# Four layers of cross-attention and feed-forward on one core: in the last attention, the reciprocal of the row sums and the scaling of the probabilities change places with the statistics of the next unit

## What is computed

```python
q = (hidden_states @ Wq).reshape(B, S, N_HEADS, HEAD_DIM)
k = (encoder_hidden_states @ Wk).reshape(B, S_enc, N_KV_HEADS, HEAD_DIM)
v = (encoder_hidden_states @ Wv).reshape(B, S_enc, N_KV_HEADS, HEAD_DIM)
q = rms_norm(q, q_norm_w)
k = rms_norm(k, k_norm_w)
...
scores = jnp.einsum('bqhd,bkhd->bhqk', q, k) * scale
probs = jax.nn.softmax(scores, axis=-1)
out = jnp.einsum('bhqk,bkhd->bqhd', probs, v)
...
return out @ Wo
```

## Time and profile before

| | us |
|---|---|
| median of 3 runs | 1542.64 |
| lowest and highest | 1542.45, 1543.8 |
| the profiled execution, first to last instruction (span) | 1540.9 |
| PE busy in it | 1443.8 (94%) |
| DVE, ACT, POOL busy | 895.8, 762.5, 528.4 |
| TensorE's granted clock, mean of the span | 0.985 |

### The profile page before, as it was taken

The page is one execution under the profiler, slowest core; times in us unless marked ns, Lnnn a source line. Parts: engine busy times, 40 slices in busy tenths (PEclk is TensorE's granted clock), DMA queues, the critical chain, the costliest instruction groups (busy, mean ns, idle before and its releaser), DMA issues. The chain is left out here.

```text
span 1540.9 us, 22220 instructions
## 1 busy us (share of the span) xinstructions
PE 1443.8 (94%) x6908; PEld 1036.8 (67%) x6910; DVE 895.8 (58%) x1940; ACT 762.5 (49%) x2116; POOL 528.4 (34%) x519
## 2 busy tenths in 40 slices
PE   4999998899999999999999999999968999999998
PEld 1677777777874555557787979776745666665656
DVE  7888988888875242323555454554686555553322
ACT  4888888888882211110343535343456555544210
POOL 2667677877761000000542424221111333321000
PEclk9999999999999999999999999999979999999999
DMA  5211000200007311112100000002141000001120
GB/s 198 80 41 59 8 5 1 94 1 1 1 1 291 144 57 48 54 49 76 66 1 1 1 0 9 20 1 83 37 181 45 1 1 1 1 29 34 51 64 21
DMA packets 21304, 71.65 MB, mean 47 GB/s; under 512 B 3859, under 2 KB 6291, under 8 KB 18245
## 3 DMA queue, kind: packets, MB, share of 16 engines
q1 hardware_dynamic: 12980, 57.37, 10.0%
q10 hardware_dynamic: 8208, 12.87, 2.6%
HBM read 69.01 MB, written 1.22 MB: 46 GB/s over the span
## 5 line engine op out<-in xcount | busy, mean ns | idle before, releaser
L1190 ACT ACTIVATE l0f_silu<-bank 128x512 f32<-128x512 f32 x48 | 28.6, 597 | 199.9 <-PE bank L1114 189.8
L828 POOL TENSOR_TENSOR l0a_stepped<-l0a_y,l0a_m 128x512 f32<-128x512 bf16 x64 | 74.0, 1156 | 94.4 <-DVE l0a_m L575 93.0
L1293 DVE TENSOR_TENSOR l0f_product<-l0f_silu,bank 128x512 f32<-128x512 f32 x48 | 32.9, 688 | 123.8 <-ACT l0f_silu L1190 123.7
L856 POOL TENSOR_TENSOR l0a_head_rstd<-l0a_head_var,all_minus_half 128x4 f32<-128x4 f32 x96 | 100.8, 1054 | 7.6 <-DVE l0a_head_var L597 7.6
L427 PEld LDWEIGHTS bank<-l0a_k_t,l0a_q_t 128*128 128x128 f32 x512 | 63.2, 191 | 49.1 <-ACT l0a_q_t L753 45.1
L767 ACT ACTIVATE l0a_work<-bank,l0a_neg_max 128x128 f32<-128x128 f32 x256 | 90.2, 370 | 0.9 <-DVE l0a_neg_max L610 0.9
L1126 PEld LDWEIGHTS bank<-all_weights_a,l0f_hidden 128*128 128x128 f32 x384 | 72.9, 190 | 25.2 <-issue 17.0
L1730 DVE TENSOR_TENSOR all_weights_a<-bank,all_cols 128x512 f32<-128x512 f32 x64 | 43.9, 690 | 77.9 <-PE bank L1559 45.9
L1126 PE MATMUL bank<-all_weights_a,l0f_hidden 128*128 128x256 f32 x384 | 88.9, 379 | 0.0
L427 PE MATMUL bank<-l0a_k_t,l0a_q_t 128*128 128x128 f32 x512 | 72.1, 284 | 17.1 <-ACT l0a_q_t L753 16.7
L2608 POOL TENSOR_TENSOR l3a_q_scale<-l3a_q_var,all_minus_half 128x4 f32<-128x4 f32 x32 | 32.4, 1013 | 159.7 <-DVE l3a_q_var L2398 159.7
(11 more groups left out here) (434 smaller groups left out, 3825.8 us busy)
## 6 DMA issues: line engine op xcount, KB each, us to landing
l0f_spread<-l0f_weights ACTq DMA_DIRECT2D x32, 192.0 KB, 2.7
all_weights_a<-in_l_w_q SPq DMA_DIRECT2D x2, 2048.0 KB, 14.5
l0f_spread<-l0f_weights ACTq DMA_DIRECT2D x32, 128.0 KB, 2.9
all_weights_b<-in_l_e_gate_up SPq DMA_DIRECT2D x1, 3200.0 KB, 10.6
all_weights_b<-in_l_e_gate SPq DMA_DIRECT2D x1, 3072.0 KB, 10.2
all_weights_a<-in_l_e_up SPq DMA_DIRECT2D x4, 768.0 KB, 7.2
all_weights_a<-in_l_e_down SPq DMA_DIRECT2D x1, 3072.0 KB, 16.8
l3a_spread<-l3f_weights SPq DMA_DIRECT2D x10, 256.0 KB, 3.5
```

The costliest lines, as they stand in the source:

```text
L828: done = g.tensor_tensor(stepped[:, 0:n], value, step, ALU.add)
L856: g.tensor_tensor(head_rstd[:, m % 2, :], head_var[:, m % 2, :], res.minus_half[:, 0:HU], ALU.pow)\
```

## The change

It edits the lists of two engines. On DVE, `row_inverse` of a unit is due one step earlier and stands between `keep_rows` and `variance` of the unit that follows it. On POOL, `scale_probs` is due one step earlier and stands ahead of `query_scale` of the unit that follows it.

```diff
--- before.py
+++ after.py
@@ -2510,7 +2510,7 @@
             keep_queries(0, 0)
             keep_rows(0, 1)
             march(VTS, STEPS, [(attention(row_max), later(UNIT, 2)), (attention(keep_queries, 1), later(UNIT, 1)),
-                               (attention(row_inverse), later(UNIT, 3)), (attention(keep_rows, 2), UNIT),
+                               (attention(keep_rows, 2), UNIT), (attention(row_inverse), later(UNIT, 2)),
                                (attention(variance, 1), UNIT), (attention(token_variance), [1]),
                                (attention(token_rows), [3]), (attention(add_to_x), [UNIT[-1] + 7]),
                                (once(F_VAR, f_variance), every), (once(F_ROWS, f_token_rows), every),
@@ -2619,7 +2619,7 @@
                 f_rows_ready.wait(g, f_rows_ready.at(t - 2, 1))
                 g.tensor_tensor(f_rstd[:, i:i + 1], f_var[:, i:i + 1], res.minus_half[:, 0:1], ALU.pow)                 .then_inc(f_rstd_ready.sem, 1)
 
-            march(VTS, STEPS, [(attention(query_scale), UNIT), (attention(scale_probs), later(UNIT, 3)),
+            march(VTS, STEPS, [(attention(scale_probs), later(UNIT, 2)), (attention(query_scale), UNIT),
                                (attention(token_rstd_of), [2]), (once(F_VAR, f_token_rstd), every)])
```

## The result

| | before | with the change |
|---|---|---|
| median, us | 1542.55 (4 runs) | 1529.99 (4 runs) |
| lowest and highest | 1541.69, 1543.8 | 1527.23, 1532.28 |
| span of the profiled execution | 1540.9 | 1530.5 |
| TensorE's granted clock in it | 0.985 | 0.985 |

The ratio is 0.9918, with a 95% interval of 0.9903 to 0.9933: faster by 12.6 us in the median, by 10.4 in the two profiled spans. The prediction had 11.9 for the gain, and 1530.7 for the median.

What follows compares the result with a forecast made beforehand. Bound: a chain leaving PE, its transposes waiting for a GpSimd scaling queued behind a power. Terms -0.5 - 9.2 - 0.9 - 1.3 = -11.9 us from the 1540.9 span, plus 1.7 to the median: 1530.7; 8-in-10 range 1528 to 1537.5.

Steps and rivals of the forecast that it cites:

- The mechanism and its price: Last attention: PE's transposes wait for a GpSimd scaling queued behind a power not needed yet; 0.43 us per plain unit.
- The plain unit: Last attention, unit without token norm: scores to next scores falls from 6.64 to 6.21 us.
- The unit with the token norm: Last attention, unit also carrying the token norm: 0.97 us of waiting goes, scores to transposes becomes 0.89, the following 5.93 stays.
- steady part: Five tiles of the last attention, from 1211.55 to 1347.73: each 1.83 us shorter, together -9.2 us.
- three more units: Units after the router's stretch, transposes waiting as in a plain unit: 0.43 us saved in each, together -1.3 us.
- The router's stretch: Where DVE's router work holds PE idle: L2441 no longer held beside a scaling, one reciprocal leaves; -0.9 us.
- The start: First units of the last attention: 1.1 us lost to a later second sum, 1.6 regained over four units; net -0.5.
- The last reciprocal: End of the last attention: it blocks the first expert chunk's two products; cost nothing, with 0.3 us of slack.
- The clock: Behind PE's idle stretch in the router's part: half clock taken to remain; if not, 1.7 us more gained.
- The sum of squares waits for the scaling: Rival, last attention: DVE's sum and POOL's scaling exclude each other; total +5.0 us, 1547.6; chance 0.09.
- PE gains only part: Rival: PE gains only its modelled idle 1.04 a tile, or a ring at 6.4 takes over; -6.7 us, 1536.0; chance 0.14.
- The wait changes its name: Rival: the queries' copy or row maxima hold the scores, so the unit stays at 6.64; 1542.8 us; chance 0.07.

Runs made afterwards that it cites:

- the kernel with the mixture first: Against the changed kernel, PE's mixture of values moved ahead of the turn, output projection behind it; 1539.65 us, ratio 0.9982 to the kernel before.

## Why the prediction was right

**The mechanism and its price.** "0.43 of a plain unit is waiting for GpSimd" held but for 0.1 of it (next paragraph), and both halves alone show that in the tiles it was the order of scaling and power. With both, no transpose waits for the scaling in any unit.

**The plain unit** was to be 0.89 + 5.32 = 6.21; it is 0.99 + 5.27 = 6.26. The step that was mis-sized is the 0.89: it came from the unit at 1299.13, whose scores had waited for nothing. The rows show it by their length, 1.06 there and 1.16 in the two units ahead of it. Where scores wait for the queries' copy, as in a plain unit they still do, the weight load isn't hidden and 0.10 is added. The unit with the token norm has 1.00 + 5.99 = 6.99 instead of 6.82. These make the tile 25.66 to 25.72 instead of 25.44, and the **steady part 8.19 instead of 9.2**. That 0.89 is what comes where the scores wait for nothing was shown by the kernel with the mixture first.

The **three more units** gained 0.26, 0.35 and 0.27 instead of 0.43 each. The premise was wrong that their transposes wait as in a plain unit. The second of them in the kernel before:

```profile
1380.37 1.16 PE L2233 MATMUL bank<-all_weights_a,l3a_q_t 128*128 128x128 f32 x8
1380.48 1.12 POOL L2614 TENSOR_TENSOR l3a_probs<-l3a_probs,l3a_row_inv 128x512 f32<-128x512 f32 x1 [0.32 <-DVE l3a_row_inv L2417]
...
1381.66 0.66 PE L2241 MATMUL bank<-all_ident,l3a_probs 128*128 128x128 f32 x4
```

The scaling had waited for its reciprocal, not for a power, and it starts 0.11 behind the scores, not 0.22 as at 1284.92. The transposes come 1.20, 1.29 and 1.21 behind the scores in these units, not 1.32. Against the 0.99 of the changed kernel that leaves 0.2, 0.3 and 0.2 of waiting, close to what was gained.

**The router's stretch** (0.96 for 0.9) came out as worked out, `token_rows` at 0.41 and L2441 at 0.19 among the readings. **The start** (0.53 for 0.5) hit by luck: its loss is 1.56 where 1.1 was taken, and 2.1 are regained where 1.6 was taken; the two errors of about 0.5 cancel. **The last reciprocal** costs 0.06 and leaves no slack where 0.3 was estimated; that the product L2493 was held for 0.33 beside the scaling is as much as what is missing.

**The clock.** That the shorter idle stretch still brings half clock was right in the first trace and in one more, and not in two others. The alternative was priced at 1.7 and measured at 1.68. It should have been a term with a chance, not a fixed one.

**The sum** was 11.9 and the profiled spans give 10.4. The median gives 12.6 and hit 1530.7 within 0.7, in part because two of the four runs lay at 1527 to 1528; in the other measurements the change had 1531.54 to 1533.19, 0.8 to 2.5 above the forecast. The mechanism accounts for the 10.4, not for the rest; that the median came so near 1530.7 is luck.

**The rivals.** *The sum of squares waits for the scaling*: it starts at 1310.88 inside the scaling and takes 0.69, and so do 29 others; no sum of the 32 is over 692 ns. This rival falls, as the first attention's 96 sums had said. The exclusion itself is real in this kernel: `token_rows` takes 1.12 to 1.14 wherever it starts beside a scaling, and L2493, which reads two tiles, 1.02 where its other 25 take 0.69. The Trainium skill ("SBUF — State Buffer", section "SBUF: two separate sides") has it as a lock between DVE and GpSimd that two-port operations and those with two SBUF inputs take; the 1.02 agrees, and so does the reduction that isn't held. *PE gains only part*: true by 1.0 of the steady 9.2, but for another reason than named; neither the modelled idle time nor a ring at 6.4 set the limit. *The wait changes its name*: it did not. PE's weight load for the scores waits for L2403 for 0.75 as it did before, and of that PE feels 0.1.

## What to carry to other kernels

When two instructions that stand in a row on one engine serve different units, look for the one whose result is wanted much later; if it stands ahead, its whole length is in the ring of the other. Moving it pays only together with what feeds the other: one half alone made the time 2 us longer, the other 13 us. And take a short gap as the target only from an instruction that starts under the same conditions as the one to be improved: here the weight load was hidden in one and not in the other, and that was most of the forecast's error.

## What the runs showed of the hardware that was not expected

- Two executions of one program with the same idle stretch of PE (2.22 and 2.24 us) went on at a clock of 0.60 and at full clock; the difference is 1.68 us. The length of the idle stretch does not tell which it will be.
- Of a DVE operation that starts beside a scaling, the rows show an end a little behind the end of the scaling, wherever it started. L2493 (0.69 alone) began 0.47 before that end and ended 0.55 behind it; `token_rows` (0.41 alone) began 0.97 before it and ended 0.15 behind it; L2441 (0.19 alone), in the kernel before, 0.97 and 0.05. Each ends 0.14 to 0.26 sooner behind the scaling than its own length would have it.
- It also goes the other way. In the kernel before, L2435 began at 1380.32, 0.16 ahead of the scaling at 1380.48, and took its 0.38; that scaling took 1.12, and the other 31 took 1.04. The kernel with POOL's half alone has one such pair too, with the same lengths.
- Where the weight load of eight matmuls is itself what a wait releases (0.75 in its row), the next group on PE follows after 0.99, and where it ran 0.11 ahead, after 0.89. PE's own row shows no idle time in either case.
